# A Perceiver block's key scratch with four slots a head, its middle part stored twice, and four loads a unit that run over the eight rows of a head outermost

## What is computed

```python
x = x + xattn(layernorm(x), ctx)          # ctx (2, 2048, 128)
q = einsum('bfd,dnh->bfnh', x_normed, wq) * 8 ** -0.5
k = einsum('btd,dnh->btnh', ctx, wk)
v = einsum('btd,dnh->btnh', ctx, wv)
weights = softmax(einsum('btnh,bfnh->bnft', k, q) + bias, axis=-1)
out = einsum('bnft,btnh->bfnh', weights, v) @ wo
x = x + self_attention(layernorm(x))
x = x + feed_forward(layernorm(x))
```

## Time and profile before

| | |
|---|---|
| median of three runs | 306.85 us |
| profiled execution, its time | 304.16 us |
| its span | 301.9 us |
| mean granted clock of TensorE | 0.983 |
| PE, DVE, ACT, POOL busy | 92%, 74%, 69%, 24% of the span |
| DMA | 33.82 MB: HBM read 20.42 MB, written 12.71 MB |
| K loads | 62 of 192 KB |
| K stores | 24: eight each of 768, 512 and 256 KB |

### The profile page before, as it was taken

One profiled execution on the slowest core, in us unless ns is written; L12 is line 12 of the kernel. 1 busy time (PEld: TensorE's weight loads), 2 busy tenths in 40 slices (PEclk: granted clock), 3 DMA queues, 4 the chain that ended last, 5 costly groups with the idle time before them and its releaser, 6 DMA issues.

```text
span 301.9 us, 10317 instructions
## 1 busy us (share of the span) xinstructions
PE 278.7 (92%) x4414; PEld 179.2 (59%) x4418; DVE 222.3 (74%) x372; ACT 207.0 (69%) x427; POOL 72.0 (24%) x143
## 2 busy tenths in 40 slices
PE   6978799979989999889999999889999999899995
PEld 5444467647666655454555666557766665436675
DVE  5875389959989984555377999889899960744583
ACT  7863288959998988813445689879989997133350
POOL 5601356411011121421022676001011030110001
PEclk9998799979999999999999999999999999999999
DMA  7993503943222291282300018623223200000000
GB/s 244 410 400 90 178 26 123 346 179 88 86 72 87 72 285 55 103 319 89 123 1 2 1 56 284 255 92 87 76 65 97 58 2 2 2 0 2 0 0 24
DMA packets 12692, 33.82 MB, mean 112 GB/s; under 512 B 1077, under 2 KB 2197, under 8 KB 12262
## 3 DMA queue, kind: packets, MB, share of 16 engines
q1 hardware_dynamic: 12596, 33.11, 32.0%
q10 hardware_dynamic: 50, 0.03, 0.0%
HBM read 20.42 MB, written 12.71 MB: 110 GB/s over the span
## 4 chain that ended last, share of the span: by engine, by line
PE 57%; DVE 14%; DMA 12%; issue 6%; ACT 6%; POOL 2%; SPq 2%; ACTq 0%; DVEq 0%; POOLq 0%
PE bank L1201 55%; DMA kpair<-k_scratch 10%; DVE mx L926 9%; DMA k_scratch<-kparts 3%; ACT probs L616 2%; SPq L303 1%; DVE s_neg L1010 1%; POOL kparts L435 1%; DVE o_rec L875 1%; DVE k_rest L883 1%; SPq L329 1%; PE bank L1581 0%; DVE xn L847 0%; DVE kparts L887 0%; ACT L737 0%
## 5 line engine op out<-in xcount | busy, mean ns | idle before, releaser
L926 DVE TENSOR_REDUCE mx<-bank 128x2 f32<-128x1024 f32 x128 | 151.6, 1216 | 21.5 <-PE bank L1201 20.4
L616 ACT ACTIVATE probs<-bank 128x512 f32<-128x512 f32 x256 | 140.0, 596 | 17.4 <-PE bank L1201 13.5
L1201 PE MATMUL bank<-probs,v_all 128*9 128x128 f32 x2048 | 80.8, 276 | 2.2 <-ACT probs L616 1.5
L1201 PE MATMUL bank<-q_exp,kpair 64*128 64x128 bf16 x1024 | 81.5, 218 | 1.1 <-ACT q_exp L539 1.1
L1201 PE MATMUL bank<-kpair,q_rows 64*128 64x512 bf16 x256 | 70.8, 388 | 9.3 <-DMA kpair<-k_scratch 7.3
L1201 PEld LDWEIGHTS bank<-q_exp,kpair 64*128 64x128 bf16 x1024 | 54.9, 94 | 28.3 <-ACT probs L616 17.1
L1201 PEld LDWEIGHTS bank<-probs,v_all 128*9 128x9 f32 x2048 | 43.6, 90 | 19.1 <-ACT probs L616 4.6
L477 POOL CAST m_rows<-negm 128x2 bf16<-128x2 f32 x32 | 6.2, 193 | 116.2 <-DVE negm L933 116.2
L1201 PEld LDWEIGHTS bank<-kpair,q_rows 64*128 64x128 bf16 x256 | 21.5, 93 | 16.3 <-DMA kpair<-k_scratch 8.8
L539 ACT ACTIVATE v_all<-bank 128x512 f32<-128x512 f32 (+1 forms) x20 | 10.6, 539 | 17.5 <-PE bank L1201 17.4
L394 POOL TENSOR_TENSOR y<-ve,mhalf 128x1 f32<-128x1 f32 (+1 forms) x10 | 5.8, 580 | 53.7 <-DVE ve L834 53.7
(11 more groups left out here) (237 smaller groups left out, 348.0 us busy)
## 6 DMA issues: line engine op xcount, KB each, us to landing
kpair<-k_scratch SPq DMA_DIRECT2D x62, 192.0 KB
k_scratch<-kparts SPq DMA_DIRECT2D x8, 768.0 KB, 4.7
k_scratch<-kparts SPq DMA_DIRECT2D x8, 512.0 KB, 6.0
ctxT_s<-in_ctxT SPq DMA_DIRECT2D x4, 512.0 KB, 8.2
mask_s<-in_mask SPq DMA_DIRECT2D x2, 1024.0 KB, 8.9
k_scratch<-kparts SPq DMA_DIRECT2D x8, 256.0 KB, 7.5
wM<-in_packM SPq DMA_DIRECT2D x1, 1728.0 KB, 9.5
wB<-in_packB SPq DMA_DIRECT2D x1, 654.0 KB, 8.9
```

Source lines behind the costliest of these rows:

```text
L616: act.activation(probs[:, j % 4, :], slot_bank(l, "b", n, j), ACT.Exp).then_inc(S("slot_free"), 1)
L926: V.tensor_reduce(mx[n % 2][:, w, :], bank[:, 2 * (w % 2):2 * (w % 2) + 2, :], AX.X, ALU.max) \
L1201: return T.matmul(out_, lhsT=lhsT, rhs=rhs, start=start, stop=stop, **kw)
```

## The change

The scratch gets four slots a head instead of six: the high part once, the middle part twice, the low part once. A group of stores writes 1, 2 and 1 slots. A head's load becomes two transfers of 24 rows: the high part's eight rows, each read three times in turn (a step of 0), and the other three slots with the eight rows outermost and the slots inside. So a unit loads with four transfers of 96 KB, and `K_LOADS` is 4. The order of the 48 rows of a head in `kpair` changes from slot by slot to row by row within each of the two groups; `k_row` gives it, and `selq` and `selk` follow. Nothing else changes on PE, DVE, ACT and POOL.

```diff
-K_LOADS = 2
+K_LOADS = 4
...
+def k_row(kp, qp, d):
+
+    return K_BASE[1] + d * 3 + (kp - 1) * 2 + qp if kp else d * 3 + qp
...
-        kscr = nc.dram_tensor("k_scratch", (2, B, len(SLOTS), H, HD, SK), BF16, kind="Internal").ap()
+        kscr = nc.dram_tensor("k_scratch", (2, B, 4, H, HD, SK), BF16, kind="Internal").ap()
...
         def load_head(eng, l, p, b, u, a):
 
-            src = kscr[l, b, :, p * 2 + a, :, :]
-            eng.dma_start(kpair[u][a * HOFF:a * HOFF + HR, :], src).then_inc(S(f"k_loaded{u}"), 16)
+            row = a * HOFF
+            high = kscr[l, b, 0, p * 2 + a, :, :].unsqueeze(1).to_broadcast([HD, 3, SK])
+            eng.dma_start(kpair[u][row:row + K_BASE[1], :], high).then_inc(S(f"k_loaded{u}"), 16)
+            rest = kscr[l, b, 1:4, p * 2 + a, :, :].rearrange("s d t -> d s t")
+            eng.dma_start(kpair[u][row + K_BASE[1]:row + HR, :], rest).then_inc(S(f"k_loaded{u}"), 16)
...
                 for kp in range(PARTS):
-                    first = K_BASE[kp] // HD
-                    dst = kscr[l, b, first:first + K_TIMES[kp], :, :, t:t + SK // 2].rearrange("s h d t -> (h d) s t")
+                    first, times = (0, 1, 3)[kp], (1, 2, 1)[kp]
+                    dst = kscr[l, b, first:first + times, :, :, t:t + SK // 2].rearrange("s h d t -> (h d) s t")
                     src = kparts[:, kp, b * SK + t:b * SK + t + SK // 2].unsqueeze(1)
-                    sp.dma_start(dst, src.to_broadcast([P, K_TIMES[kp], SK // 2])).then_inc(S(f"k_stored{b}"), 16)
+                    sp.dma_start(dst, src.to_broadcast([P, times, SK // 2])).then_inc(S(f"k_stored{b}"), 16)
...
-                selq[h * HD + d, h // 2 % 2, qp, (h % 2) * HOFF + K_BASE[kp] + qp * HD + d] = one
+                selq[h * HD + d, h // 2 % 2, qp, (h % 2) * HOFF + k_row(kp, qp, d)] = one
...
-                selk[h * HD + d, kp, h * HOFF + K_BASE[kp] + qp * HD + d] = one
+                selk[h * HD + d, kp, h * HOFF + k_row(kp, qp, d)] = one
```

## The result

| | before | changed |
|---|---|---|
| median | 305.27 us (302.24 to 308.59, 4 runs) | 292.70 us (291.77 to 293.17, 4 runs) |
| profiled execution, its span | 304.16, 301.9 us | 291.77, 289.6 us |
| mean granted clock of TensorE | 0.983 | 1.0 |
| HBM written | 12.71 MB | 8.52 MB |

The ratio is 0.966, with an interval of 0.960 to 0.972: faster, by 12.6 us where 9 were forecast. A second set of four runs of the changed kernel, beside 13 of before, gave 292.66 against 304.23.

What follows compares the result with a forecast made beforehand. Late K loads and stores, directly or through DVE waiting for PE, were taken to bound the kernel. Terms 2.8 + 3.5 + 0.7 + 2.1 = 9.1 us took 304.16 to 295.1, scaled to 297.7; forecast 297.5, range 292.5 to 304.

Steps and rivals of the forecast that it cites:

- The mechanism: K loads: engines follow the outermost count, so eight replace six, a load takes 5.25 us, 1.05 earlier, and PE's waits shrink.
- Three signs: Expected: PE not idle before unit 1, load-only stretches near 190 GB/s; issues above 0.9 us would show the prediction wrong.
- the forecast alone: The main case without its rivals: 293 to 301 us, chance 0.62.
- The start: First stores and unit 1's load, layer 0: 2.17 us of PE idle time and 0.6 of half clock go; 2.8 us.
- Unit 6: Layer 0: load lands at 59.3, before PE is ready at 60.57; DVE's idle 1.83, 1.01 and 0.62 go; 3.5 us.
- Unit 7: Layer 0, behind the second stores: they issue 1.1 us later but are 1.4 shorter, so no new wait comes.
- Unit 15: Its load need only be 0.7 us earlier, so 0.7 us is gained.
- Layer 1: Before unit 6, 0.98 us of DVE idle time, for unit 7 PE's 1.08; 2.1 us. Stores' gain there worth nothing.
- Half the gain: Rival: PE's gain only reaches the next bound, sum 4.8 us, 299.4, or 302 on the median's scale; chance 0.15.
- Six engines: Rival: loads stay on six engines, so only the stores' part comes; 302 us on the median's scale; chance 0.06.
- The fixed part in turn: Rival: each transfer pays its fixed part in turn, +0.5 us a load; 303 to 305 us, no change; chance 0.09.
- Slower: Rival: transfers do not overlap, +2.3 us a load, PE waits from unit 8 on; 324 us, decides from about +1.0; chance 0.08.

Runs made afterwards that it cites:

- busy-PE run: Against the kernel before: nine unused matmuls of 512 columns on PE ahead of its wait for unit 1 of layer 0; 303.18 us, ratio 0.997. Also called PE kept busy.
- eight engines alone: Against the kernel before: six slots still stored, each head loaded with one transfer of 48 rows, the eight rows outermost; 296.06 us, ratio 0.974.
- the stores alone: Against the kernel before: four slots stored, loads still two transfers of 48 rows, six outermost, with slot 0 read six times; 297.90 us, ratio 0.981.
- the eight transfers: Against the changed kernel: each of a unit's four transfers cut in two over the keys, same bytes and engines; 321.78 us, ratio 1.058 to the kernel before.
- sixteen engines: Against the kernel before: six slots stored, a head's 48 rows adjacent in the scratch, one transfer a head; 292.94 us, ratio 0.964.
- the 24 adjacent rows: Against the changed kernel: middle and low parts in their own scratch, a head's 24 rows adjacent; 291.38 us, ratio 0.958 to the kernel before.

## Why the prediction was right, and where it was short

**The mechanism** held: eight engines (0.52 of DMA share, 0.50 expected), an even load of 5.1 us (5.25, from 6.3), no idle time of PE matmuls at unit 6, no half clock from 60 to 67, 2.2 us of idle time before `kpair` (under 4), the loads at 3% of the chain (under 4). Three signs did not come as said: PE was still idle for 0.47 us before unit 1, a load alone moved 164 GB/s and not 190, and two issues took 1.10 and 0.96 us, above 0.9.

**The number** was short. The forecast was 297.5, 9.35 us under its median of 306.85; the change brought 12.6, down to 292.70. That is 0.2 us inside the low end of the range (292.5 to 304) and just outside the 293 to 301 given to the forecast alone. That it still lay in the range is luck.

**The start was the term mis-sized**: 2.8 us in the sum, 5.24 measured. By the table and PE's timelines it has four pieces.
- Idle time at unit 1: 2.17 to 0.47, 1.70 (2.17 forecast; the stores landed at 21.8, not 21.5).
- The half clock behind that wait: 1.59, where the step took 0.6 because "PE waited for more than this load before it". The profiled execution of the busy-PE run has 1.58 less there with the wait of the load alone filled.
- PE reaches the wait at 27.18, not at 29.13, 1.95 earlier. The step took 29.13 as a fixed time of before, and it is not one. Of it 0.45 is that unit 0 is first read at 20.67 for 21.12, and 1.50 is the half clock of 22.2 to 25.6.

The two last facts go together in ten traces. PE's pause before the first read of unit 0, which no wait of the profile ends, is 1.34 or 1.35 us in all five traces with four slots stored (two are of the changed kernel), and 1.64 to 2.12 in all five with six. Behind it half clock followed in three of those five (before, eight engines alone, PE kept busy) and in none with four slots. The kernel with the stores alone, which differs from before in nothing else of that time, has 1.35 where before has 1.94. So shorter stores shorten a pause ahead of the load's place. Why is open. Stores fill the DMA engines there, and one packet on the queue of instructions is moved near it; but before it is moved from 19.15 to 20.04, in the pause (19.17 to 21.12), and in the changed kernel from 18.17 to 19.05, ahead of the pause (19.32 to 20.67). The traces thus do not show that PE waits for it.

**Unit 6** was 3.5 and came to 3.64, though by a hair: its load landed at the moment it was read. The step kept the times of before, where its place itself moves with the start. It put the issues at 54.0 to 56.2 and the landing at 59.3; they began at 48.73 to 50.95, and the load landed at 55.00. With the 5.24 us won by then added, these are 53.97, 56.19 and 60.24. So the issues were as forecast, and the landing was 0.9 later: 4.05 us after the last issue began, where 3.1 stood.

**Unit 7** was put at nothing, and is the place of layer 0 that became critical. Its load does land earlier than before, as forecast: at 60.40, with 5.24 added 65.64, for 68.81. But PE comes to it earlier too, by the 3.64 us won at unit 6, and two of its issues took 1.10 and 0.96 us while stores filled the engines. It cost 0.39 us in this execution and nothing in the second trace of the changed kernel. With six slots stored such issues decided: the two further transfers a unit cost 2.25 us at this unit alone. Since the four slots make room for the four transfers, the two halves of the change had to be priced together.

**Unit 15** was 0.7. The gain in that place is 1.08; that it makes 0.69 with unit 7's loss, close to the forecast, is chance. **Layer 1** was 2.1 and came to 2.81, 1.40 at unit 6 (0.98 forecast) and 1.41 at unit 7 (1.08). It is not the clock, which was at 1.00 from 192.7 to 196.0 before too. The step counted idle time alone, and at unit 7 DVE's four reductions also took 4.99 us before and 4.61 after; the rest I did not trace to its parts.

**The rivals.** Half the gain: no, nothing else took over as the bound. Six engines: no, by the DMA share. The fixed part in turn: no. Four transfers took 5.1 us where two on as many engines took 4.7 to 5.1, and doubling their number to eight added 2.0 to 2.2, half a microsecond for each. The Trainium skill ("DMA: Bandwidth & Descriptors", "Anatomy of one DMA — SWDGE (gpsimd) path") gives some 2.0 us of fixed time for a transfer issued from GpSimd, while these are issued from SP; estimated from that figure four in turn would take 8.9 us. The trace agrees with a fixed latency paid once, and not with one paid by each transfer in turn. Slower: not here, but its threshold was real. It was set at a load that takes 1 us more, and the eight transfers, with 1 us more than before, took 17.6 us more.

**The sum**: 9.1 forecast, 12.4 measured in the profiled executions. Of the 3.3 us between them 2.4 are the start and 0.7 layer 1.

## What to carry to other kernels

An idle time of a microsecond or two at TensorE costs its own length and may cost as much again in the half clock behind it (1.6 us here), so a load that is just late is priced at the one with a chance of the other; and an engine's time of arrival at a wait is itself a product of what the change moves. The engines that move a transfer follow its outermost dimension, which is often had by laying out the scratch: here sixteen engines did as much as eight and a third less stored. More transfers for the same bytes cost their issues, which is nothing until the queue, above all where stores fill the engines, becomes the last to finish. Two changes that shorten the same wait do not add, and where one makes room for the other's cost they are priced together: 6.8 and 8.7 us alone, 12.6 together.

## What the runs showed of the hardware that I had not expected

- The time of an issue on SP fell with the number of engines: medians of 0.69 us for six, 0.65 for eight (with 24 rows as with 48), 0.46 for twelve, 0.42 for sixteen, all for loads of one or half a head. Twelve is what the expectation gave the 24 adjacent rows, not a share that was read; and since the two quick ones read adjacent rows, the layout may have its part.
- An issue takes up to twice as long while the engines are full of stores: 1.2 to 1.4 us in place of 0.65.
- The spread of the kernel before (301.4 to 308.6 us) goes with its granted clock: runs at 0.994 took 301.4 to 304.1 us, those at 0.978 305.9 to 307.4, one at 0.967 308.48. The changed kernel had 1.0 in all eight runs and a spread of 1.5 us. Part of what a change of this kind wins is that the long cases are gone.
- Whether half clock follows a wait was not a matter of its length alone. Leaving out the eight transfers, it followed PE's waits for a load of 1.22, 1.43, 1.60, 1.62, 2.17 and 2.20 us, and did not follow those of 1.08, 1.17, 1.49 and 1.98 us.
